# Order of the scan products on TensorE and of the first gelu halves on VectorE in a fused Mamba-style layer with a dense expert mixture

## The reference

```python
# state-space layer, 8 heads of 64, state 64
z = x @ Wz;  ssm_in = x @ Win            # -> B, C (64 each), dt (8), X (8 x 64)
delta = softplus(dt + dt_bias)
h = exp(-delta * exp(A_log)) * h + X_t * (delta * B_t);  y_t = h @ C_t
y = y + D_param * X
x = layernorm(x + (y * (silu(z) @ Wzg)) @ Wout)
# mixture; dw1, dw2, dw3: softmax over the top 3 of 12, zero elsewhere
h = gelu(sum_e dw1[:, e] * (x @ W1[e].T))          # hidden 512, exact gelu
y = sum_e dw2[:, e] * (h @ W2[e].T) + dw3 @ b2
x = layernorm(x + y)
```

## Time and profile before

| | |
|---|---|
| time, median of 3 runs | 1536.09 us (1536.03 to 1536.16) |
| time of the profiled execution | 1534.3 us |
| its span, first to last instruction | 1532.6 us |
| TensorE busy, 8646 matmul instructions | 1517.7 us (99%) |
| VectorE busy | 1115.1 us (73%) |
| ScalarE busy | 597.8 us (39%) |
| GpSimd busy | 658.1 us (43%) |
| TensorE in the chain that ended last | 92% |
| granted TensorE clock, mean | 0.999 |

### The profile page before, as it was taken

How to read it: one execution, slowest core, us unless ns; L and a number is a source line. 1 busy time by engine, 2 the same in 40 slices (tenths; PEclk the granted TensorE clock), 3 DMA queues, 4 the chain that set the end, 5 groups by cost and what they waited for, 6 DMA issues and landing times.

```text
span 1532.6 us, 25381 instructions
## 1 busy us (share of the span) xinstructions
PE 1517.7 (99%) x8646; PEld 1250.9 (82%) x8646; DVE 1115.1 (73%) x3113; ACT 597.8 (39%) x1360; POOL 658.1 (43%) x751
## 2 busy tenths in 40 slices
PE   9999999999999999999999999999999999999998
PEld 7778888888888888888788888888888888887876
DVE  7677776877768687676877768777687776867755
ACT  6643424425244351533425244252443515335130
POOL 6771624617145270643616246162451715436040
PEclk9999999999999999999999999999999999999999
DMA  5350312304022040321403123140230403214020
GB/s 178 103 150 28 117 44 68 100 29 134 19 81 87 30 138 15 106 68 49 118 22 115 45 66 102 29 130 24 74 94 29 139 15 98 77 29 134 20 76 7
DMA packets 81456, 114.53 MB, mean 75 GB/s; under 512 B 10144, under 2 KB 37296, under 8 KB 81328
## 3 DMA queue, kind: packets, MB, share of 16 engines
q1 hardware_dynamic: 81328, 112.92, 24.9%
HBM read 107.76 MB, written 5.13 MB: 74 GB/s over the span
## 4 chain that ended last, share of the span: by engine, by line
PE 92%; POOL 3%; DVE 1%; issue 1%; DMA 1%; SPq 1%; ACT 0%; POOLq 0%; DVEq 0%
PE exp_bank L247 23%; PE exp_bank L249 22%; PE exp_bank L248 22%; PE mix_bank L895 4%; PE mix_bank L938 4%; PE mix_bank L247 3%; PE mix_bank L249 3%; PE mix_bank L248 3%; PE mix_bank L920 3%; PE mix_bank L793 1%; PE turn_bank L1265 1%; PE mix_bank L525 1%; PE mix_bank L739 1%; PE mix_bank L1029 1%; POOL w_lo L445 1%
## 5 line engine op out<-in xcount | busy, mean ns | idle before, releaser
L1206 POOL TENSOR_TENSOR sp_lo<-fbuf,sp_hi 128x512 fp32r<-128x512 f32 (+2 forms) x201 | 243.3, 1214 | 194.4 <-ACT sp_hi L1202 106.6
L247 PE MATMUL exp_bank<-w_hi,sp_hi 128*128 128x512 f32 x768 | 304.1, 396 | 0.8 <-POOL sp_lo L1258 0.8
L247 PE MATMUL exp_bank<-sp_hi,w_hi 128*128 128x512 f32 x764 | 303.0, 397 | 0.9 <-POOL sp_lo L1206 0.7
L249 PE MATMUL exp_bank<-w_hi,sp_lo 128*128 128x512 f32 x768 | 299.8, 390 | 0.0
L248 PE MATMUL exp_bank<-w_lo,sp_hi 128*128 128x512 f32 x768 | 298.8, 389 | 0.0
L249 PE MATMUL exp_bank<-sp_hi,w_lo 128*128 128x512 f32 x764 | 297.8, 390 | 0.0
L248 PE MATMUL exp_bank<-sp_lo,w_hi 128*128 128x512 f32 x764 | 297.4, 389 | 0.0
L1305 DVE SCALAR_TENSOR_TENSOR acc<-exp_bank,dw,acc 128x128 f32<-128x128 f32 x384 | 132.2, 344 | 137.3 <-PE exp_bank L249 136.7
L1202 ACT CAST sp_hi<-fbuf 128x512 fp32r<-128x512 f32 (+2 forms) x203 | 120.0, 592 | 283.7 <-DVE fbuf L1172 227.7
L856 POOL TENSOR_TENSOR Wt<-Wt,Gh 128x512 f32<-128x512 f32 x128 | 184.1, 1440 | 10.2 <-DVE Wt L848 10.1
L247 PEld LDWEIGHTS exp_bank<-sp_hi,w_hi 128*128 128x128 f32 x764 | 143.4, 188 | 39.0 <-issue 8.8
(11 more groups left out here) (267 smaller groups left out, 2273.0 us busy)
## 6 DMA issues: line engine op xcount, KB each, us to landing
row_b<-dw_rows SPq DMA_DIRECT2D x189, 256.0 KB, 3.3
seg_b<-dA_rows SPq DMA_DIRECT2D x124, 256.0 KB, 3.6
ctd<-cum_rows SPq DMA_DIRECT2D x128, 96.0 KB, 3.2
x_in<-in_x SPq DMA_DIRECT2D x16, 256.0 KB, 2.7
result<-acc SPq DMA_DIRECT2D x15, 256.0 KB, 2.2
fbuf<-in_W1T SPq DMA_DIRECT2D x12, 256.0 KB, 3.8
acc<-in_W2T SPq DMA_DIRECT2D x5, 256.0 KB, 3.6
x_in<-in_W2T SPq DMA_DIRECT2D x5, 256.0 KB, 2.8
```

The costliest lines, as they stand in the source:

```text
L247: nc.tensor.matmul(ps, s_hi, m_hi, start=start and j == 0, stop=False, skip_group_check=onto)
L249: last = nc.tensor.matmul(ps, s_lo, m_hi, start=False, stop=stop and j == n - 1, skip_group_check=onto)
L1206: sig("xw_lo", on.tensor_tensor(lo[:, cols], wide[e % 2][:, cols], hi[:, cols].bitcast(F32), ALU.subtract))
```

## The change

In `mix_y_pair` TensorE does carried 0, carried 1, within 0, within 1, in both pairs of every stage, that of batch 1 too. The carried product opens the bank (its first matmul starts the sum) and the within-chunk product closes it. The semaphore `ps_yq` is replaced by `ps_ys`, raised after a carried product. What used to wait for `ps_yq` because the row was complete now waits for `ps_yw`, which the within-chunk product raises last; what waited for it because S or `ctd` was read now waits for `ps_ys`; the gates wait for both. In the start of batch 0 the order stays within, then carried. On VectorE the gelu parts 0 and 1 come ahead of the gates of rows 2 and 3 in every stage, parts 2 and 3 behind them as before. ScalarE and GpSimd keep their order.

```diff
@@ -177,7 +177,7 @@
             ps_z=NK, tanh=NK, silu=NK, silu_hi=NK, silu_lo=NK, ps_X=NC, Xd=NC, ps_zg=NQ, zg=NQ,
             ps_dA=1, dA=1, ecum=1, ps_G=1, Gm=1, ps_ends=1, ends=1, end_dt=1, Xde=NC - 1,
             ps_st=2, state=NC - 1, st_tmp=NC - 2, ctd=NQ, scan=H, G_dt=H, W=H,
-            ps_yw=NQ, ps_yq=NQ, gated=NQ, ps_out=1, v=1,
+            ps_yw=NQ, ps_ys=NQ, gated=NQ, ps_out=1, v=1,
 
             ln1_v=7, ln1_s=2, x1=1, ps_x1T=1, x1T=1, ps_lg=1, lg=1, rt_v=8, rt_s=1, dw=1, ps_dwT=1, dwT=1,
...
@@ -725,7 +725,7 @@
 
         def start_row(b, q):
 
-            wait(SP, "ps_yq", b if q >= 2 else b.prev(), q - 1 if q >= 2 else None)
+            wait(SP, "ps_ys", b if q >= 2 else b.prev(), q - 1 if q >= 2 else None)
             for j in range(2):
                 sig(f"ctd_in{q % 2}", SP.dma_start(ctd[j * NS:(j + 1) * NS, q % 2, :],
...
@@ -798,7 +798,7 @@
                 for c, (use, at, k) in enumerate(place):
                     ps = bank_of(use, b)[:, at:at + N]
                     wait(DVE, "ps_st", b, k)
-                    wait(DVE, "ps_yq", b.prev())
+                    wait(DVE, "ps_ys", b.prev())
                     if c == 0:
                         sig("state", DVE.tensor_copy(S[:, 0, :], ps))
...
@@ -884,47 +884,48 @@
                         PE.matmul(ps[j * HD:(j + 1) * HD, tok(c)], Xd[:, c, h * HD:(h + 1) * HD],
                                   row_b[h // NC][:, tok(h % NC)], start=(c == 0), stop=False)
 
-        def mix_y_within(b, q):
-
-            ps = mix_bank(b, f"y{q}")
+        def mix_y_within(b, q, opens):
+
+            ps = mix_bank(b, f"y{q}") if opens else bank_of(f"y{q}", b)
             wait(PE, "W", b, 2 * q + 2)
             for c in range(NC):
                 for j in range(2):
                     h = 2 * q + j
                     at = j * T + c * P
                     last = PE.matmul(ps[j * HD:(j + 1) * HD, tok(c)], Xd[:, c, h * HD:(h + 1) * HD],
-                                     Wt[:, q % 2, at:at + P], start=(c == 0 and not first(b)), stop=False)
+                                     Wt[:, q % 2, at:at + P], start=False, stop=not opens and c == NC - 1)
             sig("ps_yw", last)
 
+        def mix_y_carried(b, q, opens):
+
+            ps = mix_bank(b, f"y{q}") if opens else bank_of(f"y{q}", b)
+            wait(PE, "state", b)
+            wait(PE, "ctd", b, q + 1)
+            alone(PE)
+            for c in range(1, NC):
+                for j in range(2):
+                    n = slice(j * NS, (j + 1) * NS)
+                    last = PE.matmul(ps[j * HD:(j + 1) * HD, tok(c)], S[n, c - 1, q * HD:(q + 1) * HD],
+                                     ctd[n, q % 2, (c - 1) * P:c * P], start=opens and c == 1, stop=not opens and c == NC - 1)
+            sig("ps_ys", last)
+
         def mix_y_pair(eng, b, q):
 
             if eng is PE:
-                mix_y_within(b, q)
-                if b.off == 1:
-                    mix_y(PE, b, q)
-                mix_y_within(b, q + 1)
-            if eng is not PE or b.off > 1:
-                mix_y(eng, b, q)
+                mix_y_carried(b, q, True)
+                mix_y_carried(b, q + 1, True)
+                mix_y_within(b, q, False)
+                mix_y_within(b, q + 1, False)
+            mix_y(eng, b, q)
             mix_y(eng, b, q + 1)
 
         def mix_y(eng, b, q):
 
-            if eng is PE:
-                ps = bank_of(f"y{q}", b)
-                wait(PE, "state", b)
-                wait(PE, "ctd", b, q + 1)
-                alone(PE)
-                for c in range(1, NC):
-                    for j in range(2):
-                        n = slice(j * NS, (j + 1) * NS)
-                        last = PE.matmul(ps[j * HD:(j + 1) * HD, tok(c)], S[n, c - 1, q * HD:(q + 1) * HD],
-                                         ctd[n, q % 2, (c - 1) * P:c * P],
-                                         start=False, stop=c == NC - 1)
-                sig("ps_yq", last)
             if eng is SP and q + 2 < NQ:
                 start_row(b, q + 2)
             if eng is DVE:
-                wait(DVE, "ps_yq", b, q + 1)
+                wait(DVE, "ps_yw", b, q + 1)
+                wait(DVE, "ps_ys", b, q + 1)
                 wait(DVE, "zg", b, q + 1)
                 sig("gated", DVE.tensor_tensor(zg[:, q, :], bank_of(f"y{q}", b)[:, :], zg[:, q, :], ALU.mult))
...
@@ -1227,9 +1228,10 @@
                 if e < E - 1:
                     sig("ps_h", last)
 
-        def expert_gelu(eng, b):
-
-            for i, k in enumerate(hidden(b)):
+        def expert_gelu(eng, b, part=range(NH)):
+
+            for i in part:
+                k = hidden(b)[i]
                 g = zg[:, k, :] if last_batch(b) else wide[k % 2]
                 if eng is AC:
...
@@ -1436,8 +1438,10 @@
                     SP.wait_ge(sems["w_lo0"], rests(NW - 3))
                     SP.wait_ge(sems["w_lo1"], rests(NW - 1))
                 mix_load_next(eng, p)
+            if eng is DVE:
+                expert_gelu(DVE, p, range(2))
             mix_y_pair(eng, b, 2)
-            expert_gelu(eng, p)
+            expert_gelu(eng, p, range(2, NH) if eng is DVE else range(NH))
             if not norm_before:
                 second_weights_ready(eng)
```

More of the change, by code:

```diff
@@ L507, in mix_x @@
                 wait(AC, "ps_xT", b)
-                wait(AC, "ps_X" if early else "ps_yq", b.prev())
+                wait(AC, "ps_X" if early else "ps_yw", b.prev())
                 if 0 in parts:
@@ L515, in mix_x @@
                 wait(DVE, "xT", b)
-                wait(DVE, "ps_X" if early else "ps_yq", b.prev())
+                wait(DVE, "ps_X" if early else "ps_yw", b.prev())
                 sig("xT_lo", DVE.tensor_tensor(xT_lo[:, :], xT[:, :], xT_hi[:, :].bitcast(F32), ALU.subtract))
@@ L627, in mix_z @@
                     wait(AC, "ps_z", b, k + 1)
-                    wait(AC, "ps_yq", b.prev(), NQ - 1)
+                    wait(AC, "ps_yw", b.prev(), NQ - 1)
                     sig("tanh", AC.activation(silu[:, k, :], bank_of(f"z{k}", b)[:, :], ACT.Tanh, scale=0.5))
@@ L654, in mix_X @@
                     wait(on, "ps_X", b, c + 1)
-                    wait(on, "ps_yq", b.prev())
+                    wait(on, "ps_yw", b.prev())
                     sig("Xd", (AC.copy if on is AC else DVE.tensor_copy)(Xd[:, c, :], bank_of(f"X{c}", b)[:, :]))
@@ L1511, in start_pe @@
             mix_y_skip(PE, b, 0)
-            mix_y_within(b, 0)
-            mix_y(PE, b, 0)
+            mix_y_within(b, 0, True)
+            mix_y_carried(b, 0, False)
             mix_y_skip(PE, b, 1)
             mix_dt(PE, nxt)
-            mix_y_within(b, 1)
-            mix_y(PE, b, 1)
+            mix_y_within(b, 1, True)
+            mix_y_carried(b, 1, False)
             mix_bc(PE, nxt)
             mix_y_skip(PE, b, 2)
-            mix_y_within(b, 2)
-            mix_y(PE, b, 2)
+            mix_y_within(b, 2, True)
+            mix_y_carried(b, 2, False)
             mix_z(PE, nxt)
             mix_y_skip(PE, b, 3)
-            mix_y_within(b, 3)
-            mix_y(PE, b, 3)
+            mix_y_within(b, 3, True)
+            mix_y_carried(b, 3, False)
             mix_X(PE, nxt, [0])
```

## The result

The changed kernel takes 1539.95 us in the median of 10 runs (1537.81 to 1542.11), the kernel before 1536.12 us beside it (10 runs, 1535.22 to 1540.57). The ratio is 1.0021, with an interval of 1.0013 to 1.0029: 3.8 us slower. The predicted 1538.0 us is 2 us short, inside the range.

The account below looks back on a forecast made before the run. TensorE was taken as the bound, busy 1517.7 of 1532.6 us. The profiled 1534.3 - 1.5 - 0.2 + 3.7 gave 1536.3 us; with the median 1.8 us above the profiled execution, the forecast was 1538.0 us, range 1534.2 to 1540.8.

Parts of the forecast that it names:

- Part 1: In first pairs of batches 2 to 15, TensorE's new products' order makes the decay product timely: 1.53 us gained.
- the late input of batch 8: At the last expert, POOL's half of the input came late in the batch shown; 0.2 us counted as gained.
- the input of expert 9: Behind the first pair, POOL's subtraction for expert 9 comes 0.8 us later; slack falls from 2.0 to 1.2 us, costing nothing.
- Part 2: In batches 2 to 15, two gelu halves ahead of the gates on VectorE fit into idle time: 0 us.
- Rival (b): In each later batch the second cast is caught behind POOL's subtraction: 4.2 us more, 1542.2 us; chance 0.08.
- Part 3: In batch 1 the gates stand behind the moved gelu halves, so the output product starts 3.7 us later.
- Rival (a): TensorE's clock falls in the new gap of batch 1: 1.7 us more, 1539.7 us; chance 0.15.
- The prediction's own sign of being wrong: On TensorE in batch 1, a granted clock under 1.00 near 119 us would show the forecast wrong.
- no instruction is added: In the products' order on TensorE, a pair issues 32 within and 24 carried instructions before and after.
- I count this at nothing, because TensorE waits again: Batch 1's first pair is shortened by 0.8 us of carried product put into a 1.2 us wait; counted at nothing.
- (c): Batch 1 pays nothing, since the gates do not bind or the weight chain shortens as much: 1534.4 us; chance 0.09.
- (d): Entering each pair with the carried part is cheaper, 28 times, 1.4 to 2.8 us in all; chance 0.08.

Follow-up runs that it names:

- Kernel 5: The kernel before with only the two gelu halves moved ahead of the gates, from batch 2 on, old products' order; ratio 1.0003.
- kernel 6: kernel 1 with a third cast ahead of the gates in batches 2 to 15; 1537.98 us, ratio 1.0018 to the kernel before.
- kernel 3: The kernel before with only the gelu halves moved, in all batches, old products' order; 1540.80 us, ratio 1.0034.
- kernel 11: The changed kernel run once more, unaltered; 1539.00 us, ratio 1.0026 to the kernel before.
- kernel 4: The changed kernel with twelve idle TensorE products ahead of the bias product in batch 1; 1537.92 us, ratio 1.0015 to the kernel before.
- kernel 12: kernel 1 with 54 empty instructions between TensorE's expert products of batch 0, shifting its code; 1532.25 us, ratio 0.9981 to the kernel before.
- kernel 1: The changed kernel with the gelu halves moved only from batch 2 on, batch 1 keeping gates first; 1534.17 us, ratio 0.9992 to the kernel before.
- kernel 10: kernel 1 with TensorE's batch 1 wait for the last weights put behind the output product; 1534.50 us, ratio 0.9993 to the kernel before.

## Why the prediction came out as it did

**Part 1, -1.5 us: right.** All 14 first pairs are at 1.97 us, the sum is 27.54 us. From batch 2 on it is 1.69 us in the trace, against the 1.7 forecast, which is partly luck: the late input of batch 8 that the prediction counted as gained (0.2 us) is gone, but three batches between 845 and 1126 us are now 0.1 to 0.2 us longer than the others. The scan of the fifth head waits for the pair's end as said (its idle time grew from 0.63 us to 2.10), and the input of expert 9 came 0.8 to 0.9 us later, with about 1 us to spare where 1.2 were forecast. No product waited for it.

**Part 2, 0 us: right.** Kernel 5 measures it alone at 1.0003, and kernel 6 shows that one cast more is too much. Rival (b) did not occur: the two casts take 0.76 us in all 14 batches.

**Part 3, +3.7 us: right in size and place.** The gates hold the output product by 3.80 us (3.71 in kernel 3).

**Rival (a), the clock, priced at +1.7: it occurred.** 1.63 us in the profile of after and of kernel 3, and 2.5 in kernel 11. I gave it 0.15, on the ground that the fall need not come at the distance of the earlier trace rows. The tail's 3.5 us without work and the 3.7 us of my own sum lay next to each other; these rows bore a chance of a half or more. The prediction's own sign of being wrong, a granted clock under 1.00 near 119 us, is there. With this rival the sum would have been 1539.7, 0.3 us from the measured median; that it comes so near is partly luck, since two terms of the next paragraph are missing from it. TensorE: Matmul & The Clock Gate (What's actually happening) in the Trainium skill, by whose rule this rival was possible, agrees so far as that: the clock fell in the profiles of after and of kernels 3, 4 and 11, behind idle time each time.

**The step that failed: "no instruction is added" taken to mean that nothing but TensorE's order moves.** I looked at what the last weights of batch 1 wait for, and not at what shares the DMA engines with them. The new order shifted the fetch of TensorE's code by 0.8 to 1.4 us, counted from their issue, into the weight transfers and made the bias product 1.4 us later. The sum lacked this term. The gain ahead of it was missed as well. "I count this at nothing, because TensorE waits again" does not hold, since the last weights are issued earlier too, the first of the three transfers 17.15 to 17.42 us after the first pair of batch 1 in the ten profiles with the new order, 17.74 to 18.22 in the four with the old, and the second pair starts 18.63 to 19.13 us after the first instead of 19.15 to 19.90. In after against before that is -0.65 us. Part 1 in batch 1 was counted at 0 and is +1.39 - 0.65. With the packet out of the way (kernel 12) only the gain is left: its first pair of batch 2 starts 1.14 us earlier than before (0.38 us of it already at the first pair of batch 1), and the time is 2.8 us under before.

**Rivals (c) and (d).** (c) is out, batch 1 pays. (d) is out: the entry out of the 512-column stream is 0.32 us in both orders, and the undisturbed pair 3.355 us in both.

**The interval.** The measured time lies inside the range, and the mechanism of its largest term was right, but the 2 us between 1538.0 and 1539.95 are a clock fall that was given 0.15 and two terms that were counted at nothing and partly cancel. 0.13 to 0.29% slower lies across the bound of 0.2%, so "same" and "slower" were about equally right. The chances of 0.69 and 0.26 leaned too far to "same", for the reason given under (a).

## What to carry to other kernels

When a call is moved ahead of another in a loop, price the first iteration by itself: its engines wait for other things (here the loading of weights), and work that is free behind a full pipeline lands there on the path. A gap on TensorE costs more than its length, as the clock may fall and the next products run at half speed; put the gaps of the trace that show a fall beside the one that is being made, and do not count on their length alone: here one of 2.39 us had no fall, and another execution had one 2.1 us into a gap. Where a critical transfer changes its landing time although its issue did not move, look in the transfer view for the instruction queue's packets: here 54 empty instructions moved one of them away. And before two profiles are compared at one place, compare them at a place ahead of the change: here they already differ by up to 1.6 us at the first pair of batch 1.

## What the runs showed of the hardware that was not expected

- A 16 KB code packet of 0.96 us among three 256 KB transfers delays the landing of the second by 1.1 to 1.9 us (4.2 to 4.8 us in nine profiles against 2.9 to 3.1 us in five). Of 224 writes of 24 KB none with an instruction packet that started 0.5 to 1.1 us behind the issue landed on time (1.4 to 1.5 us), and all 68 late ones had such a packet within 0.5 to 1.7 us: 2.9 to 3.7 us to landing with 16 KB, 1.7 to 2.6 us with 8 KB.
- The granted clock fell after 3.61 us without TensorE work (kernel 3), at 116.7 in the changed kernel after 2.3 us, a bias product of 1.1 us and 0.3 us more of idle time, at 115.0 in its second profile (kernel 11), 2.1 us into a gap of 2.3 us, and at 116.0 in kernel 4 while idle products ran. It did not fall in gaps of 2.39 us (kernel 1) and 2.22 us (kernel 10). It stayed at 0.50 for 3.4 us (kernels 3 and 4), 6.8 us and 10.2 us (the changed kernel).
